# A Fourier layer's sweep with squares from a moment matrix, an inverse y product on 32-row blocks, and a new order of work

## The reference, cut to what matters

```python
x_ft = jnp.fft.rfft2(v)
out1 = jnp.einsum('bixy,ioxy->boxy', x_ft[:, :, :M1, :M2], W1)      # M1 = M2 = 12
out2 = jnp.einsum('bixy,ioxy->boxy', x_ft[:, :, -M1:, :M2], W2)
x1 = jnp.fft.irfft2(out_ft, s=(Sx, Sy))                             # other modes are zero
x2 = jnp.einsum('bcxy,cd->bdxy', v, w_w[i]) + w_b[i][None, :, None, None]
v = x1 + x2
mean, var = jnp.mean(v, axis=(0, 2, 3)), jnp.var(v, axis=(0, 2, 3))
v = (v - mean) * jax.lax.rsqrt(var + BN_EPS) * bn_g[i] + bn_b[i]
if i < L - 1: v = jax.nn.relu(v)
```

## Time and profile before

| | us |
|---|---|
| runs: median (lowest to highest of 3) | 3385.28 (3376.81 to 3389.48) |
| profiled execution, its span | 3381.9 |
| TensorE busy with matmuls | 2785.4 |
| TensorE busy with weight loads | 1477.3 |
| VectorE busy | 2119.0 |
| ScalarE busy | 1400.7 |
| GpSimd busy | 638.6 |

### The profile page before, as it was taken

How to read it: one execution, slowest core, us unless ns; L and a number is a source line. 1 busy time by engine, 2 the same in 40 slices (tenths; PEclk the granted TensorE clock), 3 DMA queues, 4 the chain that set the end, 5 groups by cost and what they waited for, 6 DMA issues and landing times. The chain is left out here.

```text
span 3381.9 us, 104377 instructions
## 1 busy us (share of the span) xinstructions
PE 2785.4 (82%) x45316; PEld 1477.3 (44%) x45316; DVE 2119.0 (63%) x3067; ACT 1400.7 (41%) x2298; POOL 638.6 (19%) x806
## 2 busy tenths in 40 slices
PE   3589999988999999699999975825488852999999
PEld 1245555544555555355555531202266640333333
DVE  4567777766787777667777761035467653555555
ACT  2545555545555555445555541011011110666665
POOL 3003332110233311014341100000145520000000
PEclk9779989888999999899999997967777766999999
DMA  5066666654888887288888745951122203566775
GB/s 164 18 153 147 142 139 145 139 138 128 264 266 259 249 253 201 93 269 256 253 258 257 242 143 218 430 140 38 54 62 65 67 18 68 96 120 119 120 120 91
DMA packets 243990, 541.22 MB, mean 160 GB/s; under 512 B 77857, under 2 KB 124705, under 8 KB 229953
## 3 DMA queue, kind: packets, MB, share of 16 engines
q1 hardware_dynamic: 229664, 527.43, 56.8%
q10 hardware_dynamic: 13920, 7.72, 1.1%
HBM read 320.28 MB, written 214.78 MB: 158 GB/s over the span
## 5 line engine op out<-in xcount | busy, mean ns | idle before, releaser
L838 ACT ACTIVATE p_v<-p_ps,k_scale_bias 128x1024 f32<-128x1024 f32 x384 | 446.6, 1201 | 635.3 <-PE p_ps L947 635.1
L707 DVE STREAM_TRANSPOSE p_t<-p_ps 128x1024 f32<-128x1024 f32 x192 | 363.7, 1968 | 305.8 <-PE p_ps L700 305.4
L822 POOL COPY k_xm<-p_sp 64x288 f32<-64x288 f32 x384 | 268.8, 700 | 1453.4 <-DVE p_sp L301 1436.7
L947 PEld LDWEIGHTS p_ps<-k_idfty,p_t 64*128 64x128 f32 x6144 | 403.6, 206 | 182.5 <-issue 182.5
L845 ACT ACTIVATE p_ps<-p_ps 128x1024 f32<-128x1024 f32 x384 | 388.3, 1011 | 168.3 <-PE p_ps L963 167.9
L947 PE MATMUL p_ps<-k_idfty,p_t 64*128 64x128 f32 x6144 | 445.8, 299 | 14.7 <-issue 14.7
L291 DVE STREAM_TRANSPOSE p_vt<-p_v 128x1024 f32<-128x1024 f32 x384 | 448.2, 1208 | 0.0
L2065 DVE TENSOR_TENSOR x_ht<-x_ht,x_mask 128x384 f32<-128x384 f32 x512 | 268.6, 556 | 247.2 <-ACT x_ht L2039 244.2
L2039 ACT ACTIVATE x_ht<-x_ph,x_b 128x384 f32<-128x384 f32 x576 | 303.3, 578 | 195.3 <-PE x_ph L2086 195.3
L938 PE MATMUL p_ps<-p_v,k_wbd 32*32 32x512 f32 x4096 | 298.2, 607 | 21.7 <-DVE p_t L707 10.4
L2086 PE MATMUL x_ph<-x_et,x_w 64*128 64x384 f32 x1152 | 266.3, 540 | 35.7 <-DMA x_b<-in_L_ffn_b1p_dram 34.5
(11 more groups left out here) (298 smaller groups left out, 3114.3 us busy)
## 6 DMA issues: line engine op xcount, KB each, us to landing
field<-p_v SPq DMA_DIRECT2D x768, 256.0 KB, 4.6
p_v<-field SPq DMA_DIRECT2D x64, 2048.0 KB
x_mask<-expert_weights SPq DMA_DIRECT2D x32, 1536.0 KB, 13.9
l_v<-field SPq DMA_DIRECT2D x16, 2048.0 KB, 25.9
k_xm<-field SPq DMA_DIRECT2D x12, 2048.0 KB, 24.7
k_mixw<-in_L_tok_fw_dram SPq DMA_DIRECT2D x16, 1152.0 KB, 10.4
at_cf<-state_coefficients SPq DMA_DIRECT2D x32, 384.0 KB
k_mixw<-field SPq DMA_DIRECT2D x4, 2048.0 KB, 23.7
```

Source lines behind the costliest of these rows:

```text
L707: return nc.vector.transpose(st[:, q].rearrange("p x c -> p c x"), ps[:, 2 * q:2 * q + 2, :].rearrange("p j (m c) -> p c j m", c=C))
L822: nc.gpsimd.tensor_copy(view[64 * k:64 * k + 64, :, j, :, G * i:G * i + G], sp[64 * j:64 * j + 64, :, :, 16 * k:16 * k + M1].rearrange("p ...
L838: nc.scalar.activation(field[:, 2 * q:2 * q + 2, CH * half:CH * half + CH], ps[:, e, 2 * q:2 * q + 2, :], ACT.Relu, bias=bias, scale=scale ...
L947: ins = nc.tensor.matmul(ps[:, e, 2 * q + h, col:col + 128], lines, K["idfty"][rows, :], start=False, stop=True, skip_group_check=True)
```

## The change

Four things change in `layer_phase`. First, the channel products and their squares are gone. In their place TensorE makes, for each group, a 32 x 32 matrix of channel moments from the turned pixels p_vt (`gram_product`: 128 matmuls, each a block of 128 rows by 32 columns times itself, in four partition quarters of one bank), VectorE adds it to a running sum k_gacc (`gram_sum`), and in the next layer one product of that sum with four copies of the channel weights (k_wall, loaded by four new DMAs, `dense_weights`), an elementwise product and a product with ones give the squares' sum. Second, the inverse y product (`inverse_y`) uses blocks of 32 rows, 64 matmuls a half with 64 weight columns and 64 moving columns; idfty no longer has zeros. For that p_t gets another layout (`turn_inverse` writes pairs of neighbouring words) and `inverse_x` makes 32 matmuls of 32 weight columns where it made 16 of 64. Third, the pixel products loop over banks innermost and wait once at their start. Fourth, TensorE, VectorE and ScalarE have another order: both halves of group i together, each in its own set of banks.

```diff
@@ mix_vector, mix_tensor (not in the first layer)
+        dve.wait_ge(s.gw_done, 1)
+        ve.tensor_tensor(K["gw"][:, :], zb[0:C, 1, 1, 0:P], K["wall"][0:C, :], ALU.mult).then_inc(s.gw_ready, 1)
...
+        pe.wait_ge(s.wall_in, 64)
+        nc.tensor.matmul(zb[0:C, 1, 1, 0:P], K["gacc"][:, :], K["wall"][:, :], start=True, stop=True).then_inc(s.gw_done, 1)
...
+        if n == 1 and not first:
+            pe.wait_ge(s.gw_ready, 1)
@@ norm_vector, norm_tensor
-        c.then(ve.tensor_reduce(t[:, 1:2], K["zs"][:, 0:4 * n], AX.X, ALU.add))
-        c.then(ve.tensor_tensor(t[:, 0:1], t[:, 0:1], t[:, 1:2], ALU.add))
+        nc.tensor.matmul(ps[:, 0:1], K["gw"][:, :], K["one"][:, :], start=True, stop=False)
@@ inverse_x
-        for h in range(2):
-            for j in range(2):
+        for j in range(2):
+            for g in range(G):
                 rows = slice(64 * j, 64 * j + 64)
-                ins = nc.tensor.matmul(ps[64 * h:64 * h + 64, 2 * q + j, 192 * t:192 * t + 192], K["idftx"][rows, t, :],
-                                       yt[rows, :, 2 * q + h, :], start=True, stop=True)
+                ins = nc.tensor.matmul(ps[C * g:C * g + C, 2 * s + j, 192 * t:192 * t + 192], K["idftx"][rows, t, C * s:C * s + C],
+                                       yt[rows, :, g, :], start=True, stop=True)
@@ new functions
+def inverse_y(nc, K, ps, st, half):
+    for d in range(2):
+        for b in range(4):
+            for a1 in range(2):
+                for g in range(G):
+                    rows, col = slice(C * g, C * g + C), 256 * d + S * b
+                    lines = st[rows, half, 8 * d + 2 * b:8 * d + 2 * b + 2, :, a1].rearrange("p x c -> p (x c)")
+                    ins = nc.tensor.matmul(ps[64 * a1:64 * a1 + 64, g, col:col + S], lines, K["idfty"][rows, :],
+                                           start=False, stop=True, skip_group_check=True)
+    return ins
+def gram_product(nc, ps, vt):
+    for k in range(P):
+        block = vt[:, k // 32, C * (k % 32):C * (k % 32) + C]
+        ins = nc.tensor.matmul(ps[C * (k % 4):C * (k % 4) + C, :], block, block, start=(k < 4), stop=(k >= P - 4))
+    return ins
+def dense_weights(eng, s, K, par, layer):
+    for q in range(4):
+        src = par["w_w"][layer].rearrange("c (o d) -> c o d", o=1).broadcast_to([C, G, C])
+        eng.dma_start(K["wall"][C * q:C * q + C, :].rearrange("p (o d) -> p o d", o=G), src).then_inc(s.wall_in, 16)
@@ layer_phase, SP
+                dense_weights(eng, s, K, par, layer)
                 for i in range(3):
                     load(i)
...
+            eng.wait_ge(s.next_in, 64)
@@ layer_phase, VectorE
-            for i in range(n):
+            for i in range(n + 1):
                 e = i % 2
                 if i >= 1:
                     pixels_turn(i - 1, 1)
                 if i + 1 < n:
-                    inverse_turn(i + 1, 1 - e)
+                    spectrum_turn(i + 1)
                 if i >= 1:
                     rows_turn(i - 1, e)
-                pixels_turn(i, 0)
+                if i + 1 < n:
+                    inverse_turn(i + 1, 1 - e)
+                if i < n:
+                    pixels_turn(i, 0)
                 if i >= 1:
                     modes_turn(i - 1, e)
-                if i + 2 < n:
-                    spectrum_turn(i + 2)
+                    gram_sum(i - 1, e)
@@ layer_phase, TensorE: the sweep, whole
+            for i in range(n + 1):
+                e = i % 2
+                if i < n:
+                    pixels(i, e, 0)
+                    pixels(i, 1 - e, 1)
+                if i >= 1:
+                    y_product(i - 1, e)
+                if i + 1 < n:
+                    spectrum(i + 1, 1 - e)
+                if i >= 1:
+                    moments(i - 1, e)
+                    x_product(i - 1, e)
```

More of the change, by code:

```diff
@@ L625, in mix_tensor, with norm_vector @@
         ins.then_inc(s.mix_done, 1)
-def norm_vector(nc, dve, s, K, B, n, first, scale_bias, w, t, st, ones, ps):
+def norm_vector(nc, dve, s, K, B, first, scale_bias, w, t, st, ones, ps):
     ve = nc.vector
@@ L689, in norm_tensor, with inverse_x @@
         nc.tensor.matmul(ps[:, 3:6], ones[:, :], K["gram"][:, 0:3], start=True, stop=True)
-    nc.tensor.matmul(ps[:, 0:1], K["groupsum"][:, :], t[:, 0:1], start=True, stop=True)
+    else:
+        pe.wait_ge(s.gw_ready, 1)
+        nc.tensor.matmul(ps[:, 0:1], K["gw"][:, :], K["one"][:, :], start=True, stop=False)
+    nc.tensor.matmul(ps[:, 0:1], K["groupsum"][:, :], t[:, 0:1], start=first, stop=True)
     nc.tensor.matmul(ps[:, 1:3], K["groupsum"][0:C, :], st[:, 6:8], start=True, stop=True).then_inc(s.pe_step, 1)
-def inverse_x(nc, K, ps, yt, q):
+def inverse_x(nc, K, ps, yt, s):
@@ L869, in inverse_turn @@
             def inverse_turn(i, e):
-                for q in range(2):
-                    dve.wait_ge(s.ix_done, 2 * i + q + 1)
-                    at_least(dve, s.um_done, 4 * i)
-                    turn_inverse(nc, st, ps[:, e], q).then_inc(s.t_ready, 1)
+                for half in range(2):
+                    dve.wait_ge(s.ix_done, 2 * i + half + 1)
+                    if i >= 1:
+                        dve.wait_ge(s.um_done, 2 * (i - 1) + half + 1)
+                    turn_inverse(nc, st, ps[:, e], half).then_inc(s.t_ready, 1)
             def rows_turn(i, e):
@@ L890, in modes_turn, with gram_sum @@
                 turn_modes(nc, sp, ps[:, e]).then_inc(s.sp_ready, 1)
+            def gram_sum(i, e):
+                moments, total = ps[:, e, 0, 256:256 + C], K["gacc"][:, :]
+                if i == 0:
+                    ve.tensor_copy(total, moments).then_inc(s.gm_ready, 1)
+                else:
+                    dve.wait_ge(s.gm_ready, i)
+                    ve.tensor_tensor(total, total, moments, ALU.add).then_inc(s.gm_ready, 1)
             mix_vector(nc, dve, s, K, M, first, raw)
@@ L939, in pixels @@
                                          start=True, stop=False, skip_group_check=True)
-                for q in range(2):
-                    for d in range(2):
-                        for b1 in range(2):
-                            for h in range(2):
-                                x = 16 * b1 + 4 * (2 * half + d)
-                                rows, col = slice(64 * h, 64 * h + 64), 256 * d + 128 * b1
-                                lines = st[rows, q, x:x + 4, :].rearrange("p a c -> p (a c)")
-                                ins = nc.tensor.matmul(ps[:, e, 2 * q + h, col:col + 128], lines, K["idfty"][rows, :],
-                                                       start=False, stop=True, skip_group_check=True)
-                    ins.then_inc(s.um_done, 1)
@@ L951, in channels @@
-            def channels(i, e, half):
-                for a in range(4):
-                    if half == 1:
-                        pe.wait_ge(s.uo_ready, 4 * i + 2 + a // 2 + 1)
-                    elif i + 1 < n:
-                        pe.wait_ge(s.uo_ready, 4 * (i + 1) + a // 2 + 1)
-                    else:
-                        pe.wait_ge(s.sq_done, 4 * (i - 1) + 2 + a // 2 + 1)
-                    if a == 0:
-                        pe.nop(nofuse=True)
-                    for g in range(G):
-                        rows, col = slice(C * a, C * a + C), 1024 * g + CH * half
-                        ins = nc.tensor.matmul(ps[C * g:C * g + C, e, a, :], K["wbd"][rows, 1, rows], v[rows, i % 3, col:col + CH],
-                                               start=True, stop=True)
-                    if a % 2 == 1:
-                        ins.then_inc(s.zq_done, 1)
+                inverse_y(nc, K, ps[:, e], st, half).then_inc(s.um_done, 1)
@@ L992, in _ @@
                 pe.wait_ge(s.w_in, 64)
-            pixels(0, 0, 0)
-            pe.wait_ge(s.aggr, 2)
-            pe.wait_ge(s.next_in, 64)
-            for i in range(n):
+            for i in range(n + 1):
                 e = i % 2
+                if i < n:
+                    pixels(i, e, 0)
+                    pixels(i, 1 - e, 1)
                 if i >= 1:
-                    at_least(pe, s.sp_ready, i - 1)
-                    channels(i - 1, 1 - e, 1)
-                pixels(i, e, 1)
+                    y_product(i - 1, e)
                 if i + 1 < n:
```

97 lines of the change are left out of this document (40 added, 57 removed).

## The result

The changed kernel takes 4436.28 us (median of 4 runs, 4421.92 to 4444.23) against 3387.38 us, a ratio of 1.310 (95% interval 1.307 to 1.314). The profiled execution spans 4442.4 us, 1060.5 us more than before. I had predicted 3995 us and 3640 to 4350: the sign, the place and the mechanism are right, and the time is above the range.

What follows compares the result with a forecast made beforehand. TensorE, 82% busy, bounds the kernel before; after the change its code fetch would. Groups of 22.4, 24.0 and 24.0 us add 614 us to the sweeps; with +13, -18 and 3 for the runs, 3995 us, range 3640 to 4350.

Steps and rivals of the forecast that it cites:

- One block costs about 3.5 us, and the fetch sets the pace: TensorE in the sweeps: fetching each 256 instructions takes at least 3.5 us, however short their work, and hides the work.
- The first rival: Sweeps: code fetch stays hidden, TensorE and VectorE set a group of about 13.3 us; 3046 us, 10% faster; chance 0.11.
- first failing term: Sweep groups: 1546 instructions and waits, 6.04 blocks at 3.5 us, make 21.1 us a group before lateness.
- Second failing term: Code packets late beside loads and stores: 0.8 us on 3.6 blocks, 2.9 us a group in layers 1 and 2, 1.3 in layer 0.
- my 2197: The three sweeps, first to last eviction, at 22.4, 24.0 and 24.0 us a group: 2197 us against 1583.
- Between the sweeps, -5 us: Outside the sweeps' evictions: +13 us for new weight loads and -18 us for shorter drains.
- The wait for the four dense_weights DMAs: Before each first mixing product, TensorE waits 4.4 us for four new DMAs; three phases, +13 us.
- third failing term: Sweep ends: one group drains where one and a half do, -6 us in each, -18 us.
- Work: Sweep groups: TensorE's work becomes 12 us and VectorE's 11.4 to 12.9, hidden under the code fetch.
- The inverse turn: VectorE's inverse turn, writing pairs of words, costs between 1968 and 1209 ns; the better end saves 1.5 us a group.
- The sum of the moments: New VectorE step in each group: between nothing and 1209 ns, taken as 0.2 us.
- The far rival: Sweeps: most blocks late, or TensorE's clock at half level; 27 us a group, 4320 us; chance of over 4300: 0.12.

Runs made afterwards that it cites:

- e4: The changed kernel without loads of groups 3 to 31 and stores of groups 0 to 30 in the sweeps of layers 1 and 2; 4089 us.
- e2: The changed kernel with each inverse y product as 128 matmuls of 32 weight columns instead of 64 of 64; 5143 us.
- e3: The changed kernel with only 4 of a group's 128 moment matmuls, scaled by 32; 3722 us.
- e11: The kernel before with 64 extra matmuls of 32 by 32 weights and one moving column ahead of each channel product, overwritten by it; 4154 us.
- e1: The changed kernel with each inverse y product as 32 matmuls of 128 weight columns instead of 64 of 64; 4250 us.
- e14: The changed kernel with moment matmuls moving 64 columns instead of 32, and without most loads and stores in the sweeps of layers 1 and 2; 4066 us.
- e13: The changed kernel with each moment matmul moving 64 columns instead of 32, at the same instruction count; 4378 us.
- e15: The changed kernel with pixel products of 4 rows instead of 32 in layers 1 and 2 too; 4379 us.
- e12: The changed kernel with 4 of 128 moment matmuls and without most loads and stores in the sweeps of layers 1 and 2; 3421 us.
- e7: The kernel before with only the inverse turn writing pairs of words and inverse x constants reordered for it; 3355 us, ratio 0.990.
- e16: The kernel before with the paired inverse turn, without the loads and stores in the sweeps of layers 1 and 2; 3253 us.

## Why the prediction was right in sign and short in size

- **One block costs about 3.5 us, and the fetch sets the pace.** Right. In the undisturbed block of e4 it is 3.75 us, in the step from the changed kernel to e2 3.5. In none of the traces do two code packets start less than 3.10 us apart, or four in a row within less than 9.98 us, 3.33 each. The first rival (fetch hidden) falls with e2, e3 and e11, and a block with little work isn't done sooner: 1.17 us of work stand beside 3.75 in e4. The size of a block, 256 instructions or 16.4 KB, stands as inferred (256 a packet from the changed kernel to e1, to e2 and from the kernel before to e11).
- **The sum of the groups, first failing term: 21.1 us for 6.04 blocks without lateness.** Measured 22.6 to 23.1 (e4, e14). I took the fastest spacing for each block, but from one code packet of e4's layer 1 to the next it is 3.78 us at the median and 3.89 in the mean, and, as I read it, no block gives back what a longer one takes. e11 bears this out: 16.5 us for 2.8 blocks nearly leave room for two more at 3.5 us, and yet two blocks of short work cost their full 3.7 us each. About +1.7 us a group, 93 x 1.7 = 158 us.
- **Second failing term: +0.8 us on 3.6 blocks, 2.9 us a group in layers 1 and 2 and 1.3 in layer 0.** Measured 5.2 in layers 1 and 2 (28.2 against 23.0 without transfers), 0.9 us in the mean over all six blocks, and up to 2.9 in layer 0. I had seen a packet move 4.8 us late and averaged it down; the one shown above came 2.5 us late. The misses are 62 x 2.3 + 31 x 1.6 = 192 us. With the first term 350 of the 386 us by which the sweeps went over my 2197.
- **Between the sweeps, -5 us.** Measured +59.7. The wait for the four dense_weights DMAs is as forecast: TensorE stands between the last forward x of a layer and its next product for 10.1, 14.1 and 8.6 us instead of 5.4, 9.0 and 5.6, together 12.7 more against my 13. The tails are wrong, and this is the third failing term: I gave them -18, and 59.7 less 12.7 leaves +47. Matmuls of the changed kernel at the end of layer 1:

```profile
2016.36 4.08 PE L272 MATMUL p_ps<-p_vt,k_dfty 32*32 32x512 f32 x64 [3.59 <-DVE p_vt L294]
2021.87 1.89 PE L747 MATMUL p_ps<-p_vt 128*32 128x32 f32 x122 [1.43 <-DVE p_at L299]
2025.31 1.93 PE L747 MATMUL p_ps<-p_vt 128*32 128x32 f32 x128 [1.55 <-issue]
2029.06 0.33 PE L747 MATMUL p_ps<-p_vt 128*32 128x32 f32 x6 [1.81 <-issue]
2029.32 2.87 PE L283 MATMUL p_ps<-p_at,k_dftx 32*64 32x192 f32 x64
...
2046.29 0.63 PE L614 MATMUL p_ps<-k_wall,k_gacc 128*32 128x128 f32 x2 [14.11 <-DMA k_wall<-in_L_tok_w_w_dram]
```

  The moments stand ahead of the last forward x and cost two blocks of code, 7.45 us (2021.87 to 2029.32), twice in a tail. From last eviction to first product with the modes it is 50.6 us where it was 27.0. I had counted groups that drain and not what draining takes.
- **Work.** The inverse turn came out at the low end of its bounds:

```profile
L726 DVE STREAM_TRANSPOSE p_t<-p_ps 128x1024 f32<-128x1024 f32 x192 | 226.4, 1214 | 43.8 <-PE p_ps L719 43.3 <-DVE k_scale_bias L697 0.2
```

  1214 ns for 1968, as fast as a turn that writes in a row (1228 for the rows turn, line 299). Why pairs are enough isn't shown; no run writes more than two words side by side in this turn. The sum of the moments takes 149 ns (I took 0.2 us). All this lies under the fetch, as said.
- **The far rival (27 us a group, late blocks or half clock)** came nearest, with 0.12. Its lower clock came true, 0.70 to 0.77, and costs 0.7 us a group at most (e13 to e15); its late packets are what happened. The chance should have gone there: the row of the worst block was known.

Differences between the kernels' other stages are small: mixing in layer 1 takes 65.4 us from first product to first eviction (1049.2 to 1114.6), as before (65.3).

## What to carry to other kernels

Count TensorE's instructions, not only its passes. Here a float32 matmul is four of them (the 16 of a pixel product stand as 32 matmuls and 32 weight loads), and each 256 more cost 3.5 us in e2 and 3.7 in e11, whose added matmuls move one column; no four code packets in a row came faster than 3.33 us each. By these runs, cutting a product into small tiles to skip zeros pays only while a stretch of 256 instructions holds more than about 4 us of work, an estimate from the 3.8 to 3.9 us a block of e4 and e12. Beside transfers the margin is smaller, since the code packets come late: here a group's 4 MB of loads and stores cost 5.2 us once the fetch was the bound (28.2 against 23.0, e4). Where the worst case of such a term stands in the trace, size it by that and not by a mean over calm stretches.

## What the runs showed of the hardware

TensorE's code came in packets of 16.4 KB, 256 instructions, and TensorE went on 2.4 us after its packet began (1528.0 to 1530.43; 2.3 and 2.4 in the kernel before). A transfer burst delays code: with the DMA engines 98% busy at 343 GB/s a packet began 3.6 us after its block was entered, against 1.15 us at the same place of e4, where they are 3% busy over the layer; over layer 1 the mean is 2.24 us with transfers (the changed kernel) and 1.35 without (e4). The granted clock hardly mattered to these kernels that wait for code: 0.67 to 0.86 (e15, the changed kernel, e13), or 0.85 to 0.97 (e4, e14), moved the group by at most 0.7 us. Even at 2.8 blocks a group the transfers hold the sweep: the kernel before with the paired turn takes 16.4 to 16.7 us a group with them (e7) and 14.9 without (e16).
